# A routed feed-forward in one Trainium2 kernel: choice of experts behind the output's add, ranks a step later, part of the sends in the next block

## The chip, the cores and the metric

The kernel runs on one core of one Trainium2 chip. The metric is the device time of one execution in microseconds, as the median of several runs. The engines are TensorE (PE), VectorE (DVE), ScalarE (ACT), GpSimd (POOL) and SyncE (SP); each runs its own program, and they meet at semaphores.

## The reference, cut to what matters

The model is a two-layer decoder on x of 4096 tokens by 128 channels. All of it is computed in one launch. The change touches its last perceptron, its last routed layer, and (in one layout) the routed layer of layer 0:

```python
# last lines of the second cross attention, x_out is its output, h a perceptron of 4*128
h = gelu(_ln(x_out, ln3_g, ln3_b) @ li2_w + li2_b)
x = x + (... + h @ li3_w + li3_b)
# the last feed-forward, 8 experts, 2 for each token, on flat = layernorm(x)
logits = flat @ Wr.T
weights, ids = top_k(logits, 2)
weights = softmax(weights)
h = einsum('nc,efc->nef', flat, W1)          # efc: 8 x 512 x 128
act = h[..., :256] * silu(h[..., 256:])
out = einsum('nec,ne->nc', einsum('nef,ecf->nec', act, W2), router_weights)
x = x + out
```

## The kernel before, in words

The 4096 tokens lie in `xres` as 32 tiles of 128 tokens (one token per partition). The last two stages are `mlp_route` (names `s5n_`, the perceptron of the cross attention and the routing of the layer that follows) and `sparse` (names `m6_` and `m_`, the routed layer itself). `sparse` also computes the routed layer of layer 0 (`m1_`), early in the program.

**`mlp_route`** works on N = 8 groups of G = 4 tiles in a loop of N + 3 steps. All five programs are written out by hand, and the order of the calls in each step is the order on the engine. A group `t` goes through it as follows. `front(t)` normalises it (DVE, with POOL's `norm.root` for the inverse root), `turn(t)` transposes it (PE), `turn_in(t)` scales it into `xT` (ACT), `hid(t)` and `out(t)` are the two dense products (PE, 8 and 32 records of the trace), the Gelu lies between them (ACT). `carry(t)` adds the residual and the bias to `xres`, and `take(t)` adds the product. `rnorm.stats`, `rnorm.root` and `rnorm.scaled` normalise the sum into `row`, the rows that are sent. `rturn(t)` and `logits(t)` give the scores of the 8 experts, `choose(t)` finds the two best (13 short DVE operations), `ranks(t)` counts by products with constant matrices how many tokens before each one chose the same expert, and `slots(t)` makes the addresses `idx` from them. Then POOL sends the group: 8 indirect DMAs (4 tiles, 2 experts) of 128 rows of 130 floats, to `sorted` in DRAM (`m6r_row` to `sorted` in the trace). In step `t` of the loop, DVE does

```python
choose(t - 3); carry(t); take(t - 1); slots(t - 3)
rnorm.stats(t - 1); norm.stats(t + 2); rnorm.scaled(t - 1); front(t + 2)
```

and PE `hid(t)`, `turn(t + 1)`, `rturn(t - 2)`, `ranks(t - 3)`, `out(t - 1)`, `logits(t - 2)`. POOL does the roots of `t - 1` and `t + 2`, then the sends of group `t - 3`; these wait for `slots(t - 3)` by the semaphore `slotted`, and for ACT's shares. `out(t - 1)` signals `take` by the semaphore `out`. At the end DVE makes from the counts a map of which 256 rows and which expert each tile of the next stage takes.

**`sparse`** waits for the map and for all 64 sends, and then runs a loop of J = 40 tiles of W = 256 rows with B = 8 buffers. SP issues for each tile the rows (`m_xin`), and its expert's `w1` and `w2` (`m_w`), once `scaled(j - 8)` has freed the buffer. PE transposes (`m_turnP`), multiplies by `w1` (`m_hidP`) and by `w2` (`m_yP`), DVE scales the result and makes its addresses (`m_to`, the last of a tile, L3230), and POOL puts it back with two indirect DMAs into `parts`, of 8192 rows of 128 floats. When all are put, SP reads `parts` back in 16 DMAs (8 groups, 2 experts), and DVE adds them to `xres`. A last block stores `xres` with one DMA of 2 MB.

Row number and token are tied by an iota: token n * 128 + p (tile n, partition p) has the row number n * 128 + p in `parts`, so that a partition's tiles lie 128 rows apart there; and the 256 rows of a tile are read as rows p and p + 128 for partition p:

```python
sp.dma_start(xin[s][:], xs[bass.ds(r, W), :].rearrange("(r p) c -> p r c", p=P)).then_inc(came[s], 16)
halves = acc[0:2 * CAP, :].rearrange("(k n p) c -> p k n c", k=2, p=P)
```

Of the kernel before, what the change touches and what calls it, by code (L numbers as in the profile page):

```python
# [22 lines left out]
CAP = NB * L  # L23

# [860 lines left out]
class Routed:  # L885
# [3 lines left out]
    def __init__(self, sc):  # L889
        self.row = sc.sb("row", [P, 2, NT, C + 2])  # L890
        self.map_row = sc.sb("map_row", [P, CAP // 128 + 8], I32)
        self.map_own = sc.sb("map_own", [P, CAP // 128 + 8], I32)
        self.sent = sc.sem("sent")
        self.map_ready = sc.sem("map_ready")


def mlp_route(nc, xres, ident, dram, tag, mtag, src, rt, store):
# [13 lines left out]
    row, map_row, map_own = rt.row, rt.map_row, rt.map_own  # L911
    with ExitStack() as ctx:
# [31 lines left out]
        idx = sc.sb("idx", [P, 2, NT], U32)  # L944
# [30 lines left out]
        def _(pool):  # L975
# [6 lines left out]
            pool.iota(row[:, :, :, C], pattern=[[CAP, 2], [P, NT]], base=0, channel_multiplier=1, **exact).then_inc(S["consts"], 1)  # L982
# [11 lines left out]
            for t in range(N + 3):  # L994
# [4 lines left out]
                if of(t, 3):  # L999
                    r = t - 3  # L1000
                    pool.wait_ge(S["doubled"], r + 1)
                    pool.wait_ge(S["shared"], 2 * r + 2)
                    pool.wait_ge(S["slotted"], r + 1)
                    for i in range(r * G, r * G + G):
                        for k in range(2):
                            nc.gpsimd.indirect_dma_start(xs, bass.IndirectOffsetOnAxis(idx[:, k, i:i + 1], 0), row[:, k, i, :],
                                                         None).then_inc(rt.sent, 16)

        @block.scalar
        def _(ac):  # L1010
# [9 lines left out]
            for t in range(N + 3):  # L1020
                if t + 1 < N:
                    turn_in(t + 1)
                if t < N:
                    wait(ac, S["out"], t - 1)
                    for c in range(H):
                        ac.wait_ge(S["hidden"], t * H + c + 1)
                        nc.scalar.activation(act[t % 2][:, c, :], hidP[c][:], ACT.Gelu, bias=b1[:, c:c + 1]).then_inc(S["acted"], 1)
                if of(t, 2):
# [6 lines left out]
                if of(t, 3):  # L1035
                    r = t - 3
# [6 lines left out]
        def _(pe):  # L1043
# [51 lines left out]
            for t in range(N + 3):  # L1095
                if t < N:
                    hid(t)
                if t + 1 < N:
# [3 lines left out]
                if of(t, 3):  # L1102
# [9 lines left out]
        def _(ve):  # L1112
# [56 lines left out]
            for t in range(N + 3):  # L1169
                if of(t, 3):  # L1170
                    choose(t - 3)
                if t < N:
                    carry(t)
# [1803 lines left out]
def sparse(nc, xres, ident, dram, tag, glu, store, src=None, rt=None):  # L2977
# [14 lines left out]
    with ExitStack() as ctx:  # L2992
# [6 lines left out]
        if not rt:  # L2999
# [49 lines left out]
                 "gated", "acted", "summed", "scaled", "added")  # L3049
# [24 lines left out]
        def _(sp):  # L3074
            if rt:
                sp.wait_ge(rt.map_ready, 2)
                sp.wait_ge(rt.sent, 16 * 2 * NT)
# [4 lines left out]
            for j, s, q, first, last in tiles(sp):  # L3082
                wait(sp, S["scaled"], j - B + 1)
                r = sp.value_load(entry(map_row, j), min_val=0, max_val=E * CAP + E * W - W)  # L3084
                e = sp.value_load(entry(map_own, j), min_val=0, max_val=E - 1)  # L3085
                sp.dma_start(xin[s][:], xs[bass.ds(r, W), :].rearrange("(r p) c -> p r c", p=P)).then_inc(came[s], 16)  # L3086
                sp.dma_start(w1[s][:], dram[tag + "w1"][:, bass.ds(e, 1), :, :].rearrange("p e k h -> p (e k) h")  # L3087
                             ).then_inc(came[s], 16)
                sp.dma_start(w2[s][:], dram[tag + "w2"][:, bass.ds(e, 1), :, :].rearrange("p e k c -> p (e k) c")  # L3089
                             ).then_inc(came[s], 16)  # L3090
# [358 lines left out]
```

## Time and profile before

| | |
|---|---|
| median of 3 runs | 3299.97 us (3291.67 to 3302.93) |
| profiled execution, own time | 3303.45 us |
| its span | 3301.6 us |
| TensorE clock granted over the span | 0.86 |
| PE busy | 2544.8 us (77%) |
| DVE busy | 2213.1 us (67%) |
| ACT busy | 1537.4 us (47%) |
| POOL busy | 899.7 us (27%) |
| 16 DMA engines | 128.30 MB, mean 39 GB/s |
| `mlp_route` (from its first product) | about 2931 to 3117 us |
| loop of the last `sparse` | 3117 to 3272 us |
| reading back, adds, store | 3272 to 3301.6 us |

The shares are means over a dozen stages that each have their own limit. The change lies in the last 370 us, and in a layout of the early routed layer (loop 880 to 1043 us, reading back to 1062 us). What counts is which wait ends last in these stretches.

### The profile page before, as it was taken

The numbers are of one execution on the slowest core, as the hardware profiler recorded it, in microseconds if no ns is written. First come the engines' busy times: TensorE is split into PE (matmuls) and PEld (weight loads), VectorE is DVE, ScalarE is ACT, GpSimd is POOL, SyncE is SP. The second block draws the span as 40 slices with busy tenths as digits, with TensorE's granted clock in tenths as the row PEclk, the third lists the DMA queues.
The fourth block names the chain that finished last, engine by engine and source line by source line (L and its number), as shares of the span: only waits on it lengthen the run. The fifth ranks groups of instructions, "written<-read, shape, count | busy, mean of one in ns | idle before, by whom it ended". The sixth has DMA issues, their size and how long they took to land. (4 is left out here: it accounts for less than half of the span.)

```text
span 3301.6 us, 52250 instructions
## 1 busy us (share of the span) xinstructions
PE 2544.8 (77%) x16201; PEld 1866.0 (57%) x16201; DVE 2213.1 (67%) x4511; ACT 1537.4 (47%) x4292; POOL 899.7 (27%) x1265
## 2 busy tenths in 40 slices
PE   3888888873296999989933797999998689977485
PEld 2555665552295666656621585666665556655374
DVE  4999999982023677766767524788886389955344
ACT  4666666631021677765522222677774245433111
POOL 4334344423453000003210411111110133314453
PEclk8888888885698999999966668999998989988697
DMA  9300000000374000000000300000000000000266
GB/s 352 125 0 0 0 0 0 0 0 22 111 222 141 1 0 0 0 7 1 0 7 0 63 1 16 1 1 0 0 0 8 16 1 0 0 8 22 68 180 179
DMA packets 107797, 128.30 MB, mean 39 GB/s; under 512 B 30281, under 2 KB 80273, under 8 KB 103570
## 3 DMA queue, kind: packets, MB, share of 16 engines
q1 hardware_dynamic: 98450, 107.66, 10.7%
q0 software_dynamic: 9216, 19.02, 1.7%
q8 instruction: 67, 1.10, 0.1%
q14 instruction: 64, 0.52, 0.1%
HBM read 69.23 MB, written 57.41 MB: 38 GB/s over the span
## 5 line engine op out<-in xcount | busy, mean ns | idle before, releaser
L676 DVE TENSOR_TENSOR_SCAN s_state<-s_decay,s_state 128x4096 f32<-128x4096 f32 x32 | 278.0, 8688 | 35.1 <-ACT s_decay L474 35.1
L572 PE MATMUL s_ysumP<-s_state,ident 128*128 128x256 f32 x1024 | 288.0, 434 | 1.4 <-DVE s_state L686 1.4
L1493 ACT ACTIVATE s5a_prob<-s5a_scoreP,s5a_nmax 128x256 f32<-128x256 f32 x512 | 235.2, 474 | 68.2 <-DVE s5a_nmax L1667 67.8
L572 PEld LDWEIGHTS s_ysumP<-s_state,ident 128*128 128x128 f32 x1024 | 217.9, 223 | 35.3 <-DVE s_state L686 1.9
L517 PE MATMUL s_bcP<-s_bc,s_sel 96*128 96x256 bf16 x768 | 152.2, 339 | 106.8 <-DVE s_state L686 93.0
L1493 ACT ACTIVATE s2s_prob<-s2s_scoreP,s2s_nmax 128x128 f32<-128x128 f32 (+1 forms) x512 | 208.2, 423 | 45.2 <-DVE s2s_nmax L1665 44.1
L474 ACT ACTIVATE s_decay<-s_delta,s_aneg 128x255 f32<-128x255 f32 x512 | 210.0, 493 | 33.1 <-DVE s_delta L653 33.0
L3141 POOL DMA_INDIRECT parts<-m_y,m_to x160 | 153.2, 957 | 170.3 <-DVE m_y L3232 136.1
L1667 DVE TENSOR_REDUCE s5a_nmax<-s5a_scoreP 128x4 f32<-128x1024 f32 x128 | 156.6, 1224 | 43.7 <-PE s5a_scoreP L1588 41.1
L517 PEld LDWEIGHTS s_bcP<-s_bc,s_sel 96*128 96x128 bf16 x768 | 82.7, 117 | 176.5 <-DVE s_state L686 125.5
L1665 DVE TENSOR_REDUCE s2s_nmax<-s2s_scoreP 128x2 f32<-128x256 f32 (+1 forms) x256 | 130.6, 552 | 63.6 <-PE s2s_scoreP L1583 59.5
L3325 PE MATMUL m_hidP<-m_xT,m_w 128*128 128x256 f32 x640 | 155.5, 387 | 0.1
L1676 DVE COPY s2s_probT<-s2s_probP 128x768 f32<-128x768 f32 x128 | 122.3, 956 | 46.5 <-PE s2s_probP L1598 46.3
L686 DVE TENSOR_TENSOR s_state<-s_state,s_bcP 128x1024 f32<-128x1024 f32 x128 | 149.3, 1217 | 3.3
L664 DVE TENSOR_TENSOR s_state<-s_bcP,s_du 128x1024 f32<-128x1024 f32 x128 | 147.6, 1217 | 1.2
L1588 PE MATMUL s5a_scoreP<-s5a_k,s5a_q 32*128 32x256 f32 x1024 | 147.7, 406 | 0.8 <-ACT s5a_k L1473 0.8
L365 POOL TENSOR_TENSOR s_pos<-s_pos,s_lost 128x512 f32<-128x512 f32 x16 | 144.6, 9038 | 1.3
L1678 DVE TENSOR_TENSOR s5a_probT<-s5a_probP,s5a_mask 128x768 f32<-128x768 f32 x128 | 122.1, 954 | 29.5 <-PE s5a_probP L1598 27.0
L3318 PE MATMUL m_turnP<-ident,m_xin 128*128 128x128 f32 x160 | 33.2, 291 | 139.9 <-DMA m_w<-in_m_w 137.8
L3288 ACT ACTIVATE m_act<-m_hidP 128x1024 f32<-128x1024 f32 x40 | 40.9, 1023 | 211.5 <-PE m_hidP L3325 195.3
L3333 PEld LDWEIGHTS m_yP<-m_w,m_act 128*128 128x128 f32 x960 | 119.2, 192 | 12.8 <-DVE m_act L3224 7.4
L3333 PE MATMUL m_yP<-m_w,m_act 128*128 128x128 f32 x960 | 120.4, 275 | 7.2 <-DVE m_act L3224 7.2
(643 smaller groups left out, 6318.4 us busy)
## 6 DMA issues: line engine op xcount, KB each, us to landing
sorted<-blank SPq DMA_DIRECT2D x32, 1105.0 KB, 28.1
m_w<-in_m_w SPq DMA_DIRECT2D x120, 256.0 KB
m_xin<-sorted SPq DMA_DIRECT2D x80, 130.0 KB
m_w<-in_m_w SPq DMA_DIRECT2D x40, 128.0 KB
m_row<-parts SPq DMA_DIRECT2D x16, 256.0 KB, 5.3
s_mats<-s_scratch SPq DMA_DIRECT2D x4, 1024.0 KB, 12.4
m6r_row<-parts SPq DMA_DIRECT2D x16, 256.0 KB, 5.1
parts<-m_y,m_to POOLq DMA_INDIRECT x160
```

The costliest lines, as they stand in the source:

```text
L474: ins = nc.scalar.activation(decay[c][:, n, 1:], delta[:, c, 1:], ACT.Exp, scale=aneg[:, c, n:n + 1])
L517: ins = nc.tensor.matmul(bcP[k % 2][:, n, :], sel[:, line + n, :], bc3[s][:], start=True, stop=True)
L572: ins = nc.tensor.matmul(ysumP[:, c, :], ident[:], state[s][:, c, n, :], start=(n == 0), stop=(n == NS - 1))
L664: ins = nc.vector.tensor_tensor(state[s][:, c, GN * g:GN * g + GN, :], bcP[g % 2][:], du[:, c:c + 1, :].to_broadcast([P, GN, L]), ALU.mult)
L676: nc.vector.tensor_tensor_scan(cells, flat(decay[c]), cells, 0.0, ALU.mult, ALU.add).then_inc(S["scanned"], 1)
L686: nc.vector.tensor_tensor(part, part, bcP[k % 2][:], ALU.mult).then_inc(S["bc_used"], 1)
L1493: ins = nc.scalar.activation(prob[i][:, h, a:b], scoreP[i][:, h, a:b], ACT.Exp, bias=nmax[:, p % 4, h, r:r + 1], accum_out=den[s][:, r, 2 ...
L1588: ins = nc.tensor.matmul(scoreP[i][:, h, a:b], q[rows_of(h), c, r * P:r * P + P], k[rows_of(h), c, :], start=True, stop=True)
L1667: ins = nc.vector.tensor_reduce(nmax[:, p % 4, :, :].rearrange("p h r -> p (h r)"), scoreP[i][:].rearrange("p h (r k) -> p (h r) k", r=2), ...
L3141: nc.gpsimd.indirect_dma_start(acc, bass.IndirectOffsetOnAxis(to[s][:, i:i + 1], 0), y[s][:, i, :], None).then_inc(put[s], 16)
L3325: ins = nc.tensor.matmul(hidP[s % 2][:, c, :], w1[s][:, c, :], xT[s % 2][:], start=True, stop=True)
L3333: ins = nc.tensor.matmul(yP[s % 2][:, i * C:i * C + C], act[s % 2][:, k, i * P:i * P + P], w2[s][:, k, :], start=(k == 0), stop=(k == HK - 1))
```

## The change

It does this:

- **DVE in `mlp_route`**: `choose(t - 3)` is moved from the step's head to behind `take(t - 1)`; `slots` works a step later, on `t - 4`, at the step's head; `carry(t)` goes to the step's end. The loop has a step more.
- **PE**: `ranks(t - 4)` and `out(t - 1)` now stand right behind `hid(t)`, `turn` and `rturn` behind them. `logits(r)` waits for `chosen(r - 1)` and no longer for `slotted(r - 1)`.
- **ACT**: the Gelu of `t` comes before `turn_in(t + 1)`, and the shares of `t - 4` take the place of those of `t - 3`.
- **POOL**: a step sends group `t - 4`. The last LATE = 2 groups, 16 sends, are taken out of the loop and sent at the head of `sparse`'s POOL program, behind the change of blocks.
- **SP in `sparse`** (the routed one alone): the weights of the first 8 tiles are issued before the wait for the sends.
- **Partition order** (both `sparse`): the token in partition p, tile n has the row number p * 32 + n, so that the four rows which a partition reads back for a group lie next to each other in DRAM; and a tile's partition p reads rows 2p and 2p + 1 (one run of 260 floats and not two of 130).
- **Store**: each group of the output is stored by a DMA of 256 KB as soon as its adds are done, inside `sparse`; the last block is gone.

```diff
+LATE = 2
...
+    def send(self, nc, xs, i):
+
+        for k in range(2):
+            nc.gpsimd.indirect_dma_start(xs, bass.IndirectOffsetOnAxis(self.idx[:, k, i:i + 1], 0), self.row[:, k, i, :],
+                                         None).then_inc(self.sent, 16)
...
-            pool.iota(row[:, :, :, C], pattern=[[CAP, 2], [P, NT]], base=0, channel_multiplier=1, **exact).then_inc(S["consts"], 1)
+            pool.iota(row[:, :, :, C], pattern=[[CAP, 2], [1, NT]], base=0, channel_multiplier=NT, **exact).then_inc(S["consts"], 1)
...
-                if of(t, 3):
-                    r = t - 3
+                if of(t, 4):
+                    r = t - 4
                     pool.wait_ge(S["doubled"], r + 1)
                     pool.wait_ge(S["shared"], 2 * r + 2)
                     pool.wait_ge(S["slotted"], r + 1)
-                    for i in range(r * G, r * G + G):
-                        for k in range(2):
-                            nc.gpsimd.indirect_dma_start(xs, bass.IndirectOffsetOnAxis(idx[:, k, i:i + 1], 0), row[:, k, i, :],
-                                                         None).then_inc(rt.sent, 16)
+                    for i in range(r * G, r * G + G if r < N - LATE else r * G):
+                        rt.send(nc, xs, i)
...
-                wait(pe, S["slotted"], r)
+                wait(pe, S["chosen"], r)
...
                 if t < N:
                     hid(t)
+                if of(t, 4):
+                    ranks(t - 4)
+                if of(t, 1):
+                    out(t - 1)
                 if t + 1 < N:
                     turn(t + 1)
                 if of(t, 2):
                     rturn(t - 2)
-                if of(t, 3):
-                    ranks(t - 3)
-                if of(t, 1):
-                    out(t - 1)
-                if of(t, 2):
                     logits(t - 2)
...
+            carry(0)
+            for t in range(N + 4):
+                if of(t, 4):
+                    slots(t - 4)
                 if of(t, 1):
                     take(t - 1)
                 if of(t, 3):
-                    slots(t - 3)
+                    choose(t - 3)
...
+                if t > 0 and t < N:
+                    carry(t)
...
                 sp.wait_ge(rt.map_ready, 2)
+                for s in range(B):
+                    weights(s, sp.value_load(entry(map_own, s), min_val=0, max_val=E - 1))
                 sp.wait_ge(rt.sent, 16 * 2 * NT)
...
+                sp.dma_start(xin[s][:], xs[bass.ds(r, W), :].rearrange("(p r) c -> p r c", p=P)).then_inc(came[s], 16)
+                if not (rt and isinstance(j, int) and j < B):
+                    weights(s, sp.value_load(entry(map_own, j), min_val=0, max_val=E - 1))
...
-            halves = acc[0:2 * CAP, :].rearrange("(k n p) c -> p k n c", k=2, p=P)
+            halves = acc[0:2 * CAP, :].rearrange("(k p n) c -> p k n c", k=2, p=P)
...
+            if final is not None:
+                tiled = final.rearrange("(t p) c -> p t c", p=P)
+                for t in range(N):
+                    sp.wait_ge(S["added"], t + 1)
+                    sp.dma_start(tiled[:, t * G:t * G + G, :], group(xres, t)).then_inc(S["stored"], 16)
+                sp.wait_ge(S["stored"], 16 * N)
...
-            if not rt:
+            if rt:
+                for i in range(NT - LATE * G, NT):
+                    rt.send(nc, xs, i)
+            else:
                 send(pool)
...
-        with nc.Block() as block:
-            @block.sync
-            def _(sp):
-                sp.dma_start(out.rearrange("(t p) c -> p t c", p=P), xres[:]).then_inc(gone, 16)
-                sp.wait_ge(gone, 16)
```

DVE in a middle step of `mlp_route` before, from the end of `choose` to the statistics of the group just taken (`outP` is the product, `found` and `idx` belong to `slots`, `s_xo` is the residual):

```order
L1150 TENSOR_TENSOR s5n_both<-s5n_hot 128x32
L1152 TENSOR_TENSOR s5n_apart<-s5n_top 128x4
L1127 TENSOR_TENSOR xres<-xres,s_xo 128x512
L1128 TENSOR_TENSOR xres<-xres,s5n_b 128x512
L1133 TENSOR_TENSOR xres<-xres,s5n_outP 128x512
L1157 TENSOR_TENSOR s5n_found<-s5n_hot,s5n_gateP 128x64
L1158 TENSOR_REDUCE s5n_at<-s5n_found 128x8
L1159 SCALAR_TENSOR_TENSOR s5n_idx<-s5n_which,s5n_at 128x2x4
L1161 TENSOR_REDUCE s5n_part<-s5n_both 128x8
L1162 TENSOR_TENSOR s5n_run<-s5n_run,s5n_part 128x8
L88 TENSOR_TENSOR s5n_r_cell<-s5n_r_cell 128x1
```

The same place in the changed kernel, where the 13 operations of `choose` stand between the add and the statistics (its middle ones are left out here):

```order
L1132 TENSOR_TENSOR xres<-xres,s5n_b 128x512
L1161 TENSOR_TENSOR s5n_found<-s5n_hot,s5n_gateP 128x64
L1162 TENSOR_REDUCE s5n_at<-s5n_found 128x8
L1163 SCALAR_TENSOR_TENSOR m6r_idx<-s5n_which,s5n_at 128x2x4
L1165 TENSOR_REDUCE s5n_part<-s5n_both 128x8
L1166 TENSOR_TENSOR s5n_run<-s5n_run,s5n_part 128x8
L1137 TENSOR_TENSOR xres<-xres,s5n_outP 128x512
L1144 TENSOR_REDUCE s5n_top<-s5n_gateP 128x4
...
L1154 TENSOR_TENSOR s5n_both<-s5n_hot 128x32
L1156 TENSOR_TENSOR s5n_apart<-s5n_top 128x4
L89 TENSOR_TENSOR s5n_r_cell<-s5n_r_cell 128x1
```

`slots` has moved ahead of the add and `choose` behind it; the statistics come after both as before. POOL from the last group's root on, before (L144 is the root, L1006 a send, L3133 the first instruction of `sparse`):

```order
L144 TENSOR_TENSOR s5n_r_rstd<-s5n_r_var,s5n_r_power 128x4
L1006 DMA sorted<-m6r_row,s5n_idx 34816x130 x24
L912 UNCONDITIONAL_BRANCH
L101 ISA
L3131 UNCONDITIONAL_BRANCH
L3133 IOTA m_spill 128x16
L3141 DMA parts<-m_y,m_to 10240x128 x80
```

and in the changed kernel:

```order
L145 TENSOR_TENSOR s5n_r_rstd<-s5n_r_var,s5n_r_power 128x4
L901 DMA sorted<-m6r_row,m6r_idx 34816x130 x16
L920 UNCONDITIONAL_BRANCH
L102 ISA
L3147 UNCONDITIONAL_BRANCH
L3149 IOTA m_spill 128x16
L901 DMA sorted<-m6r_row,m6r_idx 34816x130 x16
L3160 DMA parts<-m_y,m_to 10240x128 x80
```

After the last root 24 sends stood before the change of blocks; now 16 stand there and 16 behind it, and the group that was sent in the step before the last root is sent after it.

## Rows read from the trace of the kernel before

**Rows 1.** Windows, columns: window, length, PE, PEld, DVE, ACT, POOL, clock, DMA share, GB/s

```profile
3117.00:3272.00 155.00, 122.64 (x720) 107.35 (x720) 69.92 (x200) 24.73 (x41) 76.73 (x81) 0.94 0.58 171
880.00:1043.50 163.50, 152.11 (x1040) 142.68 (x1040) 44.60 (x160) 40.92 (x40) 76.58 (x80) 0.96 0.65 193
3271.00:3289.00 18.00, 0.00 (x0) 0.00 (x0) 9.75 (x15) 0.00 (x0) 0.00 (x0) 0.50 0.92 236
```

**Rows 2.** Timeline of a step of the perceptron with sends: start, duration, engine, line

```profile
3015.34 1.04 POOL L1006 DMA_INDIRECT sorted<-m6r_row,s5n_idx  x1 [0.18 <-issue]
...
3020.45 3.82 PE L1065 MATMUL s5n_outP<-s5n_w,s5n_act 128*128 128x128 f32 x32
...
3024.76 0.96 POOL L1006 DMA_INDIRECT sorted<-m6r_row,s5n_idx  x1 [0.30 <-issue]
...
3026.81 0.69 DVE L1133 TENSOR_TENSOR xres<-xres,s5n_outP 128x512 f32<-128x512 f32 x1 [6.24 <-remote]
```

**Rows 3.** Timeline of the first step, before any send, and the last group's add

```profile
2957.07 3.74 PE L1065 MATMUL s5n_outP<-s5n_w,s5n_act 128*128 128x128 f32 x32
...
2960.84 0.69 DVE L1133 TENSOR_TENSOR xres<-xres,s5n_outP 128x512 f32<-128x512 f32 x1 [13.68 <-PE s5n_outP L1065]
...
3076.87 0.69 DVE L1133 TENSOR_TENSOR xres<-xres,s5n_outP 128x512 f32<-128x512 f32 x1 [8.35 <-PE s5n_outP L1065]
```

**Rows 4.** Timeline of DVE and POOL between the adds of groups 4 and 5

```profile
3027.41 0.21 DVE L1157 TENSOR_TENSOR s5n_found<-s5n_hot,s5n_gateP 128x64 f32<-128x64 f32 x1
...
3028.32 0.15 DVE L88 TENSOR_TENSOR s5n_r_cell<-s5n_r_cell 128x1 f32<-128x1 f32 x1
...
3032.77 1.04 POOL L1006 DMA_INDIRECT sorted<-m6r_row,s5n_idx  x1 [0.18 <-issue]
...
3033.94 0.18 DVE L1140 TENSOR_REDUCE s5n_top<-s5n_gateP 128x4 f32<-128x32 f32 x1
...
3036.57 0.68 DVE L1127 TENSOR_TENSOR xres<-xres,s_xo 128x512 f32<-128x512 f32 x1
...
3044.26 0.69 DVE L1133 TENSOR_TENSOR xres<-xres,s5n_outP 128x512 f32<-128x512 f32 x1 [6.28 <-remote]
```

**Rows 5.** Timeline from the last send to the first tile of the last routed layer

```profile
3110.67 0.96 POOL L1006 DMA_INDIRECT sorted<-m6r_row,s5n_idx  x1 [0.31 <-issue]
...
3117.81 0.14 POOL L3133 IOTA m_spill<- 128x16 f32 x1 [6.18 <-POOLq L102]
...
3119.35 0.40 SPq L3086 DMA_DIRECT2D m_xin<-sorted  x1
...
3126.05 0.69 PE L3318 MATMUL m_turnP<-ident,m_xin 128*128 128x128 f32 x2 [2.03 <-DMA m_w<-in_m_w]
```

**Rows 6.** Timeline of the loop: DVE's last operation of tiles 11, 14, 17, 39

```profile
3173.04 0.15 DVE L3230 TENSOR_TENSOR m_to<-m_xin,m_spill 128x2 uint32<-128x2 f32 x1
...
3183.93 0.15 DVE L3230 TENSOR_TENSOR m_to<-m_xin,m_spill 128x2 uint32<-128x2 f32 x1
...
3192.84 0.15 DVE L3230 TENSOR_TENSOR m_to<-m_xin,m_spill 128x2 uint32<-128x2 f32 x1
...
3265.34 0.16 DVE L3230 TENSOR_TENSOR m_to<-m_xin,m_spill 128x2 uint32<-128x2 f32 x1 [0.54 <-issue]
```

**Rows 7.** Timeline of SP's queue: the rows of tiles 9 and 19

```profile
3145.63 0.38 SPq L3086 DMA_DIRECT2D m_xin<-sorted  x1
...
3185.01 0.38 SPq L3086 DMA_DIRECT2D m_xin<-sorted  x1
```

**Rows 8.** Timeline of the end: last put, reading back, last add, store

```profile
3269.46 0.96 POOL L3141 DMA_INDIRECT parts<-m_y,m_to  x1 [0.30 <-issue]
3271.78 12.73 SPq L3096 DMA_DIRECT2D m6r_row<-parts  x16
...
3288.94 1.42 DVE L3262 TENSOR_TENSOR xres<-xres,m6r_row 128x512 f32<-128x512 f32 x2 [0.18 <-DMA m6r_row<-parts]
3292.11 0.38 SPq L3429 DMA_DIRECT2D out<-xres  x1
```

More of the change, by code:

```diff
@@ L993, in _ @@
             pool.wait_ge(filled, 32 * BLANKS)
-            for t in range(N + 3):
+            for t in range(N + 4):
                 if of(t, 1):
@@ L1019, in _ @@
             ac.wait_ge(S["loaded"], 64)
-            for t in range(N + 3):
-                if t + 1 < N:
-                    turn_in(t + 1)
+            for t in range(N + 4):
                 if t < N:
@@ L1027, in _ @@
                         nc.scalar.activation(act[t % 2][:, c, :], hidP[c][:], ACT.Gelu, bias=b1[:, c:c + 1]).then_inc(S["acted"], 1)
+                if t + 1 < N:
+                    turn_in(t + 1)
                 if of(t, 2):
@@ L1094, in _ @@
             pe.wait_ge(S["consts"], 8)
-            for t in range(N + 3):
+            for t in range(N + 4):
                 if t < N:
                     hid(t)
+                if of(t, 4):
+                    ranks(t - 4)
+                if of(t, 1):
+                    out(t - 1)
                 if t + 1 < N:
@@ L1168, in _ @@
             ve.wait_ge(S["consts"], 8)
[L1169 to L1173, printed above, removed]
+            carry(0)
+            for t in range(N + 4):
+                if of(t, 4):
+                    slots(t - 4)
                 if of(t, 1):
@@ L2974, in layout5, with sparse @@
     return laid
-def sparse(nc, xres, ident, dram, tag, glu, store, src=None, rt=None):
+def sparse(nc, xres, ident, dram, tag, glu, store, src=None, rt=None, final=None):
     G = 4
@@ L3048, in sparse @@
                  "shares", "chosen", "ranked", "idx_ready", "map_ready", "sent", "xT_turned", "xT_ready", "hidden",
-                 "gated", "acted", "summed", "scaled", "added")
+                 "gated", "acted", "summed", "scaled", "added", "stored")
         S = {n: sc.sem(n) for n in names}
@@ L3074, in _, with weights @@
         def _(sp):
+            def weights(s, e):
+                sp.dma_start(w1[s][:], dram[tag + "w1"][:, bass.ds(e, 1), :, :].rearrange("p e k h -> p (e k) h")
+                             ).then_inc(came[s], 16)
+                sp.dma_start(w2[s][:], dram[tag + "w2"][:, bass.ds(e, 1), :, :].rearrange("p e k c -> p (e k) c")
+                             ).then_inc(came[s], 16)
             if rt:
                 sp.wait_ge(rt.map_ready, 2)
+                for s in range(B):
+                    weights(s, sp.value_load(entry(map_own, s), min_val=0, max_val=E - 1))
                 sp.wait_ge(rt.sent, 16 * 2 * NT)
@@ L3107, in send @@
                       allow_small_or_imprecise_dtypes=True).then_inc(S["consts"], 1)
-            pool.iota(row[:, :, :, C], pattern=[[CAP, 2], [P, NT]], base=0, channel_multiplier=1,
+            pool.iota(row[:, :, :, C], pattern=[[CAP, 2], [1, NT]], base=0, channel_multiplier=NT,
                       allow_small_or_imprecise_dtypes=True).then_inc(S["consts"], 1)
@@ L3374, in stage56 @@
         stage5(nc, xres, ident, dram, rt)
-        sparse(nc, xres, ident, dram, "m6_", True, dram["m6_store"], rt=rt)
+        sparse(nc, xres, ident, dram, "m6_", True, dram["m6_store"], rt=rt, final=dram["out"])
 def lay_out(i, np):
@@ L3409, in build @@
         dram["blank"] = (xs, blank, blanked, filled)
+        dram["out"] = out
         with nc.Block() as block:
```

14 lines of the change are left out of this document (3 added, 11 removed).

## The prediction

> **What bounds the kernel now.** I first read the windows of the stretches that the change touches, to see which of them is full. The early routed layer's loop is PE's: busy 152.1 of 163.5 us, with the DMA engines at 0.65 [rows 1]. The last one's loop is nobody's: PE is busy 122.6 of 155 us and the DMA engines are at 0.58 [rows 1]. The reading back is the DMA engines', at 0.92 and 236 GB/s, with PE idle [rows 1]. Then I read the timelines of the last 370 us for who waits for whom.
>
> In the perceptron the surprise is in [rows 2]. PE's product of group 4 starts at 3020.45 and is over 3.82 us later, at 3024.27, by its modelled end. DVE's add, which waits for nothing else and had been idle for 6.2 us, starts at 3026.81, 2.5 us after. What does end just before it is POOL's run of eight sends, from 3015.34 to 3024.76 + 0.96 = 3025.72. The distance from the run's end to the add is 1.09 us here, and about as much at the next two groups. With no send about, the add follows the product at once: 2957.07 + 3.74 = 2960.81, and the add is at 2960.84 [rows 3]. So I read: **the signal of a dense product is held while POOL sends back to back, and comes about 1.06 us after the run.** The step is then a chain: add, statistics, root, run of eight sends (10.38 us), 1.1 us, next add. By rows: add 3026.81, first send 3032.77 (5.96 us), add 3044.26, a step of 17.45 us [rows 2, 4]. PE and DVE have slack in it.
>
> In the loop of the last routed layer the same appears in a smaller form: between tiles 11 and 14 DVE's last operation moves by 3183.93 − 3173.04 = 10.89 us, 3.63 us a tile, and this spacing repeats to the hundredth from tile 5 on (four times); POOL puts six DMAs back to back in each such period. From tile 17 to 39 it is (3265.34 − 3192.84)/22 = 3.30 us a tile [rows 6]: there PE waits for SP's transfers, the sends have gaps, and nothing is held.
>
> **The change part by part**, against the profiled execution's own 3303.45 us, which is 3.5 us above the median of the runs.
>
> *Steps without sends (groups 0 to 3).* The sends of group 0 move a step later, so that the add of group 3 is no longer behind a run. A step's DVE work is some 11.4 us and PE's 10 to 11 us at full clock; by this the adds come at about 2960, 2969, 2979 and 2992 (three steps of 9 to 13 us). Before, the fourth came at 3009.4, after two longer steps and a run of sends. This gains 17 us, but it is gain only if the sends that follow are not what sets the end.
>
> *Steps with sends.* `choose` takes 3036.57 − 3033.94 = 2.63 us and now stands between the add and the statistics; `slots`, 3028.32 − 3027.41 = 0.91 us, leaves that place [rows 4]. From the add to the first send it is then 5.96 + 1.69 = 7.65 us, and the step 7.65 + 10.38 + 1.06 = 19.1 us where it was 17.45. In the last steps, with no statistics of a coming group, it is 17.6. From the add of group 3 at 2992.3: adds at 3011.4, 3030.5, 3048.1 and 3065.7. The last was at 3076.87 [rows 3], so 11 us are gained by here.
>
> *The end of the stage.* But now groups 4 to 7 are unsent at that add, where it was 5 to 7: 32 sends, not 24. Two groups go at once: first send at 3065.7 + 6.2 = 3071.9, end at 3092.7. The map is made in that time. The change of blocks took 3117.81 − 3111.63 = 6.2 us [rows 5], so the other 16 start at 3098.9 and, at twice the 10.38 us of a run, end at 3119.7, while before all had ended at 3111.63. SP waits for them: with a landing of 1.4 us (from the last put's end at 3270.42 to the next issue at 3271.78 [rows 8]) and a register load, rows are issued at about 3122.1, where the first was issued at 3119.35 [rows 5]. The weights are there by then (8 x 384 KB in 20 us), which saves their two issues before the second tile's rows, so the second transposes, at 3126.05 before [rows 5], are at about 3126. PE's first product stands behind them. **Sum to the first product: 0.** The 11 us and the early weights pay for 8 more sends and for a barrier that no longer covers anything but itself.
>
> *The loop.* With eight tiles of weights there SP is some 7 us ahead at tile 8. PE then doesn't wait for transfers from tile 17 on, POOL's puts stay back to back, and the pattern of 3.63 us a tile holds on: 22 x (3.63 − 3.30) = **+7 us** (bounds: −5, if the lead is simply kept to the end; +11, if it holds on from tile 8).
>
> *Partition order.* The rows of a tile come as one run of 1040 bytes in place of two of 520. In the early loop this is beside PE's work, 0 us. The reading back now has its four rows side by side in DRAM, but on the SBUF side they still land 130 floats apart. I take the runs to stay 512 bytes: 0 to −2 us early, **−1**. If they became 2048 bytes, it would be 5 us less in each of the two reads.
>
> *The store.* Last add ends 3290.36, store issued 3292.11, end 3301.6: 1.75 + 9.5 us [rows 8]. Now seven of eight parts are stored beside the reads; but the engines are 0.92 busy there [rows 1], so that 2 MB at 236 GB/s, some 8 us, push the reads. The end comes 2 to 6 us earlier: **−3.5**.
>
> Sum: 3303.45 + 0 + 7 − 1 − 3.5 = 3306; by the runs' median, **3302 us**.
>
> **Against a rule.** The rows show the add 1.1 us behind POOL's run, three times of three. The Trainium skill, SBUF — State Buffer (Who interferes with whom), says that PE and ACT never wait on anyone; only DVE and GpSimd share a port. By that rule PE's product isn't late for the sends' sake, and some other thing orders these rows; the first rival is what it would give, and the trace does not agree with it as I read it.
>
> **The rivals.**
>
> *1. The signal isn't held in the new order.* For it: short products' signals (the transposes', the ranks') get through in the middle of a run, and `out` now stands elsewhere in it. Against: three of three. The four steps with sends then take what POOL needs, two roots and the run, some 13.4 us, in place of 19.1, 19.1, 17.6 and 17.6: −20 us in front of the last 16 sends. The loop gives 0 in place of +7 (its pattern is the same thing), the ends −4.5: 3303.45 − 20 − 4.5 = 3279, by the median **3275**. A half way, held for some groups alone, gives 3280 to 3295.
>
> *2. Slower: the loop goes at the pace at which buffers come free.* In the stretch with the pattern SP's issues for tiles 9 to 19 are (3185.01 − 3145.63)/10 = 3.94 us apart [rows 7], since each waits for `scaled` of eight tiles before, and it loses its lead over PE there. If the pattern spreads and each release is late by it, tiles 8 to 39 go at 3.94 and not at the 3.33 they had: +19 in place of +7. This decides if the lead at tile 8 is eaten within ten tiles. 3303.45 + 19 − 4.5 = 3318, by the median **3314**. Against it: a tile's 658 KB, its puts included, take 2.8 us at the 236 GB/s of the reading back [rows 1].
>
> *3. It does not do what it says*: the store by groups and the partition order bring nothing (a gain of 0 for −4.5). Then 3306. It lies in the first case's range.
>
> **How the numbers follow.** About 0.3%, 10 us, is what a measurement of this kernel can tell from no change: faster is below 3290, slower above 3310. The held signal as above, with the bounds of the loop and of the ends (3290 to 3310): 0.50. Not held, or held in part: 0.33. Slower: 0.17. The likeliest case's own range is 3290 to 3309. Since the first rival has a third, the range reaches to its middle, 3272, and to 3313 at the other end. Faster 0.34, same 0.48, slower 0.18.
>
> **What would show it.** Right: adds of groups 3 to 7 some 19 us apart with each about 1.1 us behind a run's end; first product of the last routed layer within 3 us of 3126.5; tiles 3.63 us apart to the thirties; last stores issued right behind the last add. Wrong: steps with sends of 13 to 15 us, and the last routed layer starting 15 us or more earlier (rival 1); SP waiting for `scaled` with tiles 3.9 us apart (rival 2); a reading back of under 14 us (runs of 2048 bytes).

## The result and the profile after

The changed kernel takes 3274.81 us (median of 6 runs, 3269.45 to 3283.2) against 3295.82 us for the kernel before (6 runs): a ratio of 0.9945, 95% interval 0.9926 to 0.9964. That is 12 to 24 us faster, where 3302 was forecast, with no difference that a measurement can tell as the likeliest outcome. 3274.81 is where the first rival stood (3275), though not for its reason; it lies inside the forecast range (3272 to 3313) only because that range had been stretched down for this rival, so that much is luck. The profiled execution has a span of 3272.3 us (3301.6 before).

The part ahead of the perceptron is not touched but for one layout, and its length scatters from run to run: the perceptron began at 2902.7 to 2931.0 us in the 17 profiles of this study. So I count from that start (POOL's first instruction of the stage, 2931.0 before, 2925.8 after):

| us | before | after | forecast of the difference | measured |
|---|---|---|---|---|
| perceptron's start to add of group 3 | 78.4 | 55.4 | -17 | -23.0 |
| adds of group 3 to 7 | 67.5 | 66.4 | +6 | -1.1 |
| add of group 7 to first product of the last routed layer | 49.6 | 57.6 | +11 | +8.0 |
| that product to the last tile's last DVE operation | 138.8 | 136.3 | +7 | -2.5 |
| from there to the end | 36.3 | 30.7 | -3.5 | -5.6 |
| **sum** | 370.6 | 346.4 | +3.5 | **-24.2** |

The rest, 5.2 us, is the earlier start of the stage, the scatter just named. In the early routed layer reading back and adds took 18.8 us before and after.

The windows of the changed kernel, in the columns of [rows 1] and for the same three stretches (the loop of the last routed layer, that of the early one, the reading back):

```profile
3100.00:3242.00 142.00, 125.22 (x720) 110.98 (x720) 68.41 (x199) 23.34 (x40) 73.62 (x77) 0.93 0.55 163
876.80:1040.40 163.60, 152.88 (x1040) 143.20 (x1040) 44.58 (x160) 40.97 (x40) 76.83 (x80) 0.96 0.64 193
3247.00:3265.00 18.00, 0.00 (x0) 0.00 (x0) 10.60 (x16) 0.00 (x0) 0.00 (x0) 0.50 1.03 270
```

The loops have not changed their character. Beside the reading back the stores now run: 270 GB/s where there were 236.

A step with sends in the changed kernel, in the timeline; it answers to [rows 2, 4]:

```profile
2998.41 0.96 POOL L901 DMA_INDIRECT sorted<-m6r_row,m6r_idx  x1 [0.30 <-issue]
2999.07 0.69 DVE L1137 TENSOR_TENSOR xres<-xres,s5n_outP 128x512 f32<-128x512 f32 x1 [4.47 <-remote]
...
3002.13 0.19 DVE L1154 TENSOR_TENSOR s5n_both<-s5n_hot 128x32 f32<-128x32 f32 x1
...
3002.46 1.84 PE L1084 MATMUL s5n_gateP<-s5n_wr,s5n_rowT 128*128 128x8 f32 x8 [4.37 <-DVE s5n_both L1154]
...
3004.16 5.82 PE L1062 MATMUL s5n_hidP<-s5n_xT,s5n_w 128*128 128x512 f32 x8
...
3006.76 1.04 POOL L901 DMA_INDIRECT sorted<-m6r_row,m6r_idx  x1 [0.18 <-issue]
...
3010.86 3.82 PE L1070 MATMUL s5n_outP<-s5n_w,s5n_act 128*128 128x128 f32 x32
...
3014.51 0.60 PE L1055 MATMUL s5n_turnP<-ident,s5n_xn 128*128 128x128 f32 x4
...
3016.73 0.69 DVE L1137 TENSOR_TENSOR xres<-xres,s5n_outP 128x512 f32<-128x512 f32 x1 [4.68 <-remote]
...
3017.44 0.78 ACT L1019 ACTIVATE s5n_xT<-s5n_turnP,s5n_ln 128x512 f32<-128x512 f32 x1 [6.73 <-remote]
```

Read it as PE's chain: add 2999.07, `choose` ends 3002.3 with `both`, PE's `logits` had waited 4.37 us for it, `hid` stands behind `logits`, then `ranks` and the product, which ends at 3014.67 by its modelled end. Its add starts 2.06 us later, at 3016.73, during the last send of the run. So the signal is held as before. It is the signal that is late, not PE and not DVE: PE goes on to its transposes at once (3014.51), and ACT, idle for 6.73 us, sees the end of these transposes (3015.11) only at 3017.44. But `logits <- both` is the wait I had not read: **PE has no slack in this step.** With `out` directly behind `hid` and `ranks`, everything on PE's way from one add to the next is there: 0.6 (add) + 2.6 (`choose`) + 1.8 + 5.8 + 1.1 + 3.8 us, and 2 us of hold.

The end of the changed kernel, in the columns of [rows 8]:

```profile
3247.44 12.11 SPq L3106 DMA_DIRECT2D m6r_row<-parts  x16
...
3259.59 6.64 SPq L3111 DMA_DIRECT2D out<-xres  x8
...
3264.06 1.42 DVE L3281 TENSOR_TENSOR xres<-xres,m6r_row 128x512 f32<-128x512 f32 x2 [0.17 <-DMA m6r_row<-parts]
```

From the first reading DMA to the last add's end it is 18.0 us (18.6 before), so the stores cost the reads nothing that shows, and the end comes 6.8 us behind the last add, where it was 11.2. All 8 stores are issued after the 16 reads, on the same queue.

### The profile page after: what moved, and what is told of

It is laid out like the page before. It is cut to its first block and busy times, and to the rows that moved or that the text cites. A ratio compares the mean times of both kernels' runs of the same rounds, so it can differ in the third digit from the quotient of the medians.

```text
span 3272.3 us, 52245 instructions
## 1 busy us (share of the span) xinstructions
PE 2526.3 (77%) x16201; PEld 1854.9 (57%) x16201; DVE 2212.4 (68%) x4511; ACT 1538.3 (47%) x4290; POOL 901.2 (28%) x1265
## 5 line engine op out<-in xcount | busy, mean ns | idle before, releaser
L573 PEld LDWEIGHTS s_ysumP<-s_state,ident 128*128 128x128 f32 x1024 | 218.3, 224 | 35.6 <-DVE s_state L687 1.8
L3344 PE MATMUL m_hidP<-m_xT,m_w 128*128 128x256 f32 x640 | 162.0, 399 | 1.9 <-DVE m_xT L3237 1.7
L1683 DVE TENSOR_TENSOR s5a_probT<-s5a_probP,s5a_mask 128x768 f32<-128x768 f32 x128 | 122.1, 954 | 31.5 <-PE s5a_probP L1603 29.0
L3337 PE MATMUL m_turnP<-ident,m_xin 128*128 128x128 f32 x160 | 32.4, 286 | 130.9 <-DMA m_w<-in_m_w 97.4
L3344 PEld LDWEIGHTS m_hidP<-m_xT,m_w 128*128 128x128 f32 x640 | 122.2, 201 | 18.0 <-issue 2.0
```

Of the source, the lines that this page charges most:

```text
L573: ins = nc.tensor.matmul(ysumP[:, c, :], ident[:], state[s][:, c, n, :], start=(n == 0), stop=(n == NS - 1))
L3344: ins = nc.tensor.matmul(hidP[s % 2][:, c, :], w1[s][:, c, :], xT[s % 2][:], start=True, stop=True)
```

## Experiments

Fifteen kernels ran, on three chips: e1 to e4 on one (call it X), e5 to e8 on a second (Y), e9 to e15 on a third (Z). Each is compared with the kernel before on its own chip. Which chip the two kernels of the first result ran on is not on record. Stage lengths are those of the table's first rows: F is the perceptron's start to the first product of the last routed layer, L its loop, T the end. Each of these lengths is from one profile of its kernel.

### e1 to e4: which part of the change brings the gain, and the sends taken out of the loop

e1 takes the old order of the steps on all engines (ACT, POOL's three steps and the wait of `logits` for `slotted` go back with it), with all else as changed; in short form, DVE and PE:

```diff
-            carry(0)
-            for t in range(N + 4): slots(t - 4); take(t - 1); choose(t - 3) ...; carry(t)
+            for t in range(N + 3): choose(t - 3); carry(t); take(t - 1); slots(t - 3) ...
-                hid(t); ranks(t - 4); out(t - 1); turn(t + 1); rturn(t - 2); logits(t - 2)
+                hid(t); turn(t + 1); rturn(t - 2); ranks(t - 3); out(t - 1); logits(t - 2)
```

> The changed kernel with the step order of the perceptron as before (choose ahead of the add, ranks and sends three steps back, turn ahead of the product); the two late groups, early weights, rows and store as changed. Theory A (the order is the gain: it starts the steps without sends warm and lets the runs of sends begin at the fourth group's add): the first product of the last routed layer comes 20 to 23 us later than in the changed kernel, counted from the stage's start, and the whole is at or above the kernel before (3296 to 3302). Theory B (the late sends, weights and store are the gain): it stays within 6 us of the changed kernel's 3275.

> The changed kernel with no late groups (all 32 last sends ahead of the change of blocks) and the first tiles' weights issued with their rows, as before. Theory A: 16 sends end at the same distance, then 14.9 us from the last send to the first product as in the kernel before, where the changed kernel has 4.9 (block) + 5.8: +4 us to the first product. The loop 0 to +3 us longer. In all +4 to +7 us over the changed kernel. Theory B: more than +12 us.

> The changed kernel without the early weights alone. First product after the last send's end 9.6 us and not 5.8: +3.9 us; loop from first product to last tile +0 to +3 us by the lead that is lost (my prediction had said that losing the lead shortens the loop by 7).

> All eight groups sent behind the change of blocks, none in the loop. If a dense product's signal is held by sends back to back: each add follows its product within 0.1 us, and steps from the add of group 3 on take 12 to 13 us, not 17.7; the add of group 7 comes 102 us after the stage's start, not 121.8. If the signal is late for another reason (the product itself is slow in coming there): adds stay 1 to 2.5 us behind the modelled end of the product, and the steps stay over 15 us. The end is later by some 37 us in both, for 64 sends stand alone.

e2 sets `LATE = 0` and issues weights with the rows; e3 only does the latter; e4 sets `LATE = 8`.

| | median us | ratio to before, 95% | F | L | T |
|---|---|---|---|---|---|
| e1 old order | 3256.69 | 0.9966 (0.9947 to 0.9986) | 186.1 | 115.2 | 31.0 |
| e2 no late group, no early weights | 3252.09 | 0.9956 (0.9933 to 0.9978) | 175.9 | 120.5 | 30.8 |
| e3 no early weights | 3249.19 | 0.9944 (0.9922 to 0.9966) | 175.1 | 120.9 | 31.1 |
| e4 all sends late | 3301.35 (1 run) | | 229.1 | 115.7 | 31.3 |

Two expectations missed. e1 was to lose all of the gain; by the ratio it keeps more than half (0.34% of the 0.55 to 0.58% that the changed kernel gains). e3 loses 5 us in the loop against e1 and e4, which have the early weights on the same chip, where 0 to 3 were expected. The larger surprise was the chip: the kernel before takes 3267.22 us here (20 runs) and not 3296, and **in no trace of chip X is a signal of PE held.** In e3, with runs of sends, the adds of groups 3 to 7 are 16.1, 14.4, 14.4 and 12.5 us apart, each right behind its product; in e4, with no sends in the loop, 14.4, 14.4, 16.0 and 12.5. So where nothing is held, the sends don't set the step at all. My expectation of e4 (12 to 13 us a step) was a miss: without sends and without a hold the step is still over 14 us, so another chain must set it. e2 against e3 says that late groups by themselves bring 0.8 us to F: of the 4 us that e2 was to lose, and lost against e6 (175.9 and 172.2), nearly all is the weights'. They can only be issued early because sends are still to come.

### e5 to e8: both kernels on one other chip, `choose` moved, the store undone

```diff
e7:
-                if of(t, 3):
-                    choose(t - 3)
                 if of(t, 1):
                     ve.wait_ge(S["out_used"], t)
                     rnorm.stats(nc, ve, st, t - 1, lambda g: tile(xres, t - 1, g))
                 if t + 2 < N:
                     norm.stats(nc, ve, st, t + 2, lambda g: tile(src, t + 2, g))
+                if of(t, 3):
+                    choose(t - 3)
```

> The kernel before, unchanged, on the chip of this call, for its trace. The last four kernels ran on another chip than the first two, and there no signal of PE was held by POOL's runs. If this chip doesn't hold them either: adds of groups 4 to 6 within 0.1 us of the product's end, steps of some 16.5 us where they were 17.45, the last loop some 20 us shorter than 139 us. If it holds them, the trace repeats that of before within 2 us a stage.

> The changed kernel, unchanged, on the same chip as the kernel before. If the held signal is what the change works around, the gain is smaller on a chip that holds none. If the gain is in the order of the steps and in the store (theory A), first product some 16 us earlier from the stage's start and 5.5 us less at the end on either chip, 18 to 24 us in all.

> The changed kernel with choose(t - 3) moved behind the statistics of t - 1 and t + 2, so that its 2.6 us no longer stand between the add and the sends. My prediction's term: each of the four steps with sends loses up to 2.6 us, where the chain add, statistics, root, run, held signal sets the step: first product 5 to 10 us earlier. Rival: where nothing is held, PE's chain (logits wait for chosen) or DVE's own sum sets the step, and it gains under 2 us or loses.

> The changed kernel with one DMA of 2 MB in a block of its own at the end, as before, everything else as changed. From the last tile to the end 36.2 us and not 30.7 (5.5 us more). If the partition order had its part in that (rival), only 2 to 4 us more.

| | median us | ratio to before, 95% | F | L | T |
|---|---|---|---|---|---|
| e5 before | 3258.63 (1 run; 3263.36 in 25 others) | | 182.6 | 122.9 | 35.6 |
| e6 changed | 3242.82 | 0.9942 (0.9919 to 0.9964) | 172.2 | 115.8 | 30.9 |
| e7 choose later | 3260.15 | 1.0006 (0.9981 to 1.0031) | 188.1 | 116.3 | 31.5 |
| e8 one store | 3248.55 | 0.9956 (0.993 to 0.9983) | 171.9 | 115.5 | 36.0 |

Chip Y holds no signal either, and the ratio is the same as in the first result. The gain is made of other pieces: F -10.4 (some 16 were expected), L -7.1, T -4.7. e8 gives back 5.1 us of T and nothing else: that is the store's whole price, as my term had it (-3.5, 2 to 6). Against e6, e1 has an F longer by 13.9 us, and e3 one longer by 2.9 and an L longer by 5.1: the order of the steps is worth some 14 us, the early weights some 8, the store 5 (e1 and e3 are from chip X, which like Y held nothing). These are sizes from single profiles. By the ratios the three are 8, 1 and 5 us, each with an interval of some 10 us to either side, so the times alone settle none of them.

e7 tests my chain, on a chip where nothing is held. If add, statistics, root and sends set the step, 2.6 us less between add and sends must help. It costs 15.9 us in F and the whole gain in time. PE and DVE in e7, in the timeline:

```profile
3007.21 1.85 PE L1084 MATMUL s5n_gateP<-s5n_wr,s5n_rowT 128*128 128x8 f32 x8 [4.21 <-DVE s5n_both L1154]
```

```profile
3002.16 0.69 DVE L1137 TENSOR_TENSOR xres<-xres,s5n_outP 128x512 f32<-128x512 f32 x1 [2.66 <-PE s5n_outP L1070]
3006.88 0.19 DVE L1154 TENSOR_TENSOR s5n_both<-s5n_hot 128x32 f32<-128x32 f32 x1
```

The add comes at once, `both` 4.7 us later, and PE waits 4.21 us for it, where it waits 2.57 us in e6. So `choose` stands behind the add for PE's sake: `logits` writes the PSUM tile (`gateP`) that `choose` reads, hence its wait for `chosen`.

### e9 to e11: PE's wait taken away, the rows undone, the run of sends broken

```diff
e9, PE:
                 hid(t)
+                logits(t - 3)
                 ranks(t - 4)
                 out(t - 1)
                 turn(t + 1)
                 rturn(t - 2)
-                logits(t - 2)
e11, POOL:
                     for i in range(r * G, ...):
+                        if i == r * G + 3 and t < N:
+                            pool.wait_ge(S["out"], t + 1)
                         rt.send(nc, xs, i)
```

> The changed kernel with PE's logits(t - 3) right behind hid(t) in place of logits(t - 2) at the step's end. Theory C, formed after the last runs: the step is PE's own chain (product, add, choose, logits, hid, ranks, product), since logits writes the PSUM bank that choose reads and waits for it 2.6 us, and hid stands behind it and runs at half clock for the idle time. Then these 2.6 us go, hid takes 3.7 us more often, and steps from the fourth add on take 13 to 14 us (POOL's two roots and its run) in place of 14.4 to 16 (17.7 where signals are held): first product 5 to 10 us earlier. Theory of my prediction (the chain through statistics and the run of sends sets the step): no change, within 1.5 us.

> The changed kernel with tokens and rows numbered tile by tile as before, and a tile's rows read as two runs of 520 bytes. Early routed layer: loop and reading back within 1 us. Reading back of the last one: first issue to last add's end within 0.5 us of 18.0 to 18.4, if its runs are 512 bytes in both, as the packets of the changed kernel say (8192 of 512 bytes for both reads); 2 us longer if rows side by side in DRAM help. Loop 0 to +2 us for 5120 packets more.

> The changed kernel, POOL waiting for the product's signal after six of the eight sends of a run. If this chip holds signals during a run (as the first did): the signal comes some 1.1 us after the sixth send's end and not at or after the eighth's, so that adds come 1 to 1.5 us earlier in three steps. If it holds none (as the last two): adds come as in the changed kernel there (14.4 to 16 us apart), and the runs end up to 2 us later.

| chip Z | median us | ratio to before, 95% | F | L | T | adds of groups 3 to 7 apart |
|---|---|---|---|---|---|---|
| e9 logits next | 3260.12 | 0.9863 (0.9829 to 0.9897) | 162.0 | 139.9 | 32.4 | 11.3, 12.8, 12.5, 14.0 |
| e10 old rows | 3272.18 | 0.9905 (0.9877 to 0.9932) | 179.4 | 137.5 | 32.0 | 17.9, 17.7, 17.7, 13.1 |
| e11 pause | 3268.59 (1 run) | | 174.9 | 142.0 | 29.7 | 16.5, 16.4, 14.9, 12.5 |

Chip Z holds signals again, as the first traces did (before: 3298.57 us), and e10's perceptron is that of the first trace to a tenth. e10 shows that the numbering by partition brings nothing that these runs can tell: reading back to last add 18.2 us (18.0 changed, 18.6 before), the early layer's 19.1 (18.8). The packets say why: 12288 of 512 bytes in the window of reading back and store, before and after alike, and 10128 fewer in all, as 80 tiles are read in packets of 1040 bytes.

PE in e9:

```profile
2993.33 0.60 PE L1055 MATMUL s5n_turnP<-ident,s5n_xn 128*128 128x128 f32 x4
2993.77 0.60 PE L1077 MATMUL s5n_outP<-ident,m6r_row 128*128 128x128 f32 x4
2994.80 3.70 PE L1062 MATMUL s5n_hidP<-s5n_xT,s5n_w 128*128 128x512 f32 x8 [0.43 <-ACT s5n_xT L1019]
2998.34 0.95 PE L1084 MATMUL s5n_gateP<-s5n_wr,s5n_rowT 128*128 128x8 f32 x8
```

The wait is 0.43 us, `hid` takes 3.70 us where it took 5.82, and F is 17.4 us shorter than in e10, more than the 5 to 10 that I had expected. Theory C holds: **the step was PE's chain with a wait for `choose` in it**. The clock is part of it. Windows of the changed kernel (three steps with sends, then the `hid` of the step shown above) and of e9 (four steps), in the columns of [rows 1]:

```profile
2981.20:3034.50 53.30, 39.77 (x202) 29.11 (x200) 29.27 (x144) 21.97 (x33) 29.80 (x29) 0.81 0.09 31
3004.20:3009.80 5.60, 5.60 (x9) 2.36 (x10) 4.95 (x21) 3.18 (x4) 4.33 (x5) 0.62 0.04 12
```

```profile
2983.50:3027.00 43.50, 34.61 (x215) 27.25 (x213) 33.37 (x169) 23.82 (x38) 30.94 (x30) 0.92 0.11 38
```

In `hid` the granted clock is 0.62, that is, most of it is run at the lower level of 1.2 GHz (0.5); over the steps it is 0.81, with PE busy 39.8 of 53.3 us. In e9 it is 0.92, with PE busy 34.6 of 43.5 us and no wait of several us ahead of `hid`.

e11 shows that the held signal is real. POOL and DVE in e11:

```profile
2990.29 0.96 POOL L901 DMA_INDIRECT sorted<-m6r_row,m6r_idx  x1 [0.30 <-issue]
...
2992.13 0.69 DVE L1139 TENSOR_TENSOR xres<-xres,s5n_outP 128x512 f32<-128x512 f32 x1 [3.12 <-PE s5n_outP L1072]
2992.37 0.96 POOL L901 DMA_INDIRECT sorted<-m6r_row,m6r_idx  x1 [1.11 <-PE s5n_outP L1072]
```

The product ended at 2991.62, the sixth send at 2991.25. The add follows the product in 0.5 us where it took 2, and the steps are shorter by 0.6 to 2.8 us than in e10. POOL, which waits for the same signal, goes on 0.24 us after DVE.

### e12 to e15: what holds the signal, what it costs in the loop, and the best version

```diff
e13 and e15, POOL in the last loop:
                 for i in range(R):
+                    if rt and i == 1 and j + 3 <= J:
+                        pool.wait_ge(S["hidden"], j + 3)
```

> All sends behind the change of blocks once more, for a chip that holds signals. If the sends hold them: no add is late to its product by more than 0.1 us, and the adds of groups 4 to 7 come 14 to 16 us apart as on the chip that held none, not 17.7. If the product is slow by itself there: 1.8 to 2.5 us late as with sends. On a chip that holds none it repeats the earlier run and tells nothing new.

> The changed kernel; in the last loop POOL waits between a tile's two puts for PE's hidden product two tiles on. Where signals are held, runs of four to six puts can't form: the loop takes 118 to 130 us from first product to last tile and not 136 to 142. If the wait itself costs as much as the hold (rival), it stays over 135 us. Where none is held: 115 to 118 us, as without it.

> Logits behind hid once more. Theory C: steps with sends of 11 to 14 us and the first product 162 us after the stage's start on a chip that holds signals, 162 to 166 us on one that holds none (172 there without this edit).

> Both edits. Effects add: first product as in e14, loop as in e13. On a chip that holds signals 30 to 35 us below the changed kernel, on one that holds none 6 to 10 us below.

| chip Z | median us | ratio to before, 95% | F | L | T |
|---|---|---|---|---|---|
| e12 all sends late | 3335.64 (1 run) | | 235.5 | 142.2 | 31.3 |
| e13 pause in the loop | 3258.68 (1 run) | | 179.2 | 130.9 | 32.2 |
| e14 logits next, again | 3261.97 | 0.9915 (0.9885 to 0.9945) | 163.1 | 140.1 | 31.1 |
| e15 both edits | 3248.81 | 0.9877 (0.9815 to 0.994) | 161.4 | 132.0 | 30.2 |

e12 is the clean one. PE and DVE with no send about, on the chip that holds signals:

```profile
2992.19 3.82 PE L1070 MATMUL s5n_outP<-s5n_w,s5n_act 128*128 128x128 f32 x32
...
2999.44 1.03 PE L1084 MATMUL s5n_gateP<-s5n_wr,s5n_rowT 128*128 128x8 f32 x8 [2.56 <-DVE s5n_both L1154]
3000.33 5.38 PE L1062 MATMUL s5n_hidP<-s5n_xT,s5n_w 128*128 128x512 f32 x8
```

```profile
2996.04 0.69 DVE L1137 TENSOR_TENSOR xres<-xres,s5n_outP 128x512 f32<-128x512 f32 x1 [2.66 <-PE s5n_outP L1070]
```

Product's end 2996.01, add 2996.04; the adds of groups 3 to 7 are 16.0, 14.4, 16.1 and 12.5 us apart. So it is the sends that hold the signal, and on this chip they cost 1.8, 3.3, 1.7 and 0.6 us a step. The rest of the step is PE's chain, the same on all chips: e4 on chip X has steps of 14.4, 14.4, 16.0 and 12.5 us. (F is 6 us longer in e12 than in e4 for another reason: PE's hidden product comes 11.7 us behind the last send and not 5.7, the second tile's rows being late.)

The loop shows the same on a larger scale. Windows from first product to last tile: changed kernel (first trace, then chip Y), and e13:

```profile
3105.24:3241.59 136.35, 124.05 (x717) 110.20 (x716) 67.58 (x197) 23.34 (x40) 73.21 (x77) 0.94 0.56 166
```

```profile
3101.80:3217.60 115.80, 115.08 (x718) 105.82 (x716) 67.32 (x197) 23.89 (x40) 73.01 (x77) 0.99 0.67 195
```

```profile
3093.70:3224.60 130.90, 119.87 (x718) 105.89 (x716) 68.17 (x196) 23.90 (x40) 72.21 (x76) 0.99 0.56 172
```

Where nothing is held the loop is PE's, busy 115.1 of 115.8 us. Where signals are held it is 20 us longer. Here is one such tile of the changed kernel in its first trace:

```profile
3188.29 1.89 PE L3344 MATMUL m_hidP<-m_xT,m_w 128*128 128x256 f32 x8
...
3193.75 1.08 ACT L3304 ACTIVATE m_silu<-m_hidP 128x512 f32<-128x512 f32 x2 [5.69 <-PE m_hidP L3344]
```

ACT has been idle for 5.69 us and starts 3.57 us after PE's product has ended, while POOL puts six times in a row. In the traces with a hold it is only PE's signals that come late: in the loop ACT starts up to 3.7 us after a product that it waits for, but DVE never more than 0.12 us after ACT, and PE never more than 0.13 us after DVE. e13 wins back 5 to 11 us of that (130.9 against 136.3 to 142.2 in the other traces of changed kernels with a hold), less than the 6 to 24 that I had expected: runs of three to six puts still form, and signals are still held by up to 2.5 us. e15 adds both edits and has the lowest median of all on chip Z, 0.9877 of the kernel before. By the ratio e9, measured against other runs of the kernel before, stands no worse (0.9863), and the intervals overlap. e15 is 26 us below the first result's 3274.81, where 30 to 35 were expected. Its interval and e14's overlap, so that in time alone the loop's part isn't settled, though the stage's length says 8 us (132.0 against 140.1).

## Why the prediction was wrong

**The step that failed** is the chain of a step with sends: "The step is then a chain: add, statistics, root, run of eight sends (10.38 us), 1.1 us, next add ... PE and DVE have slack in it." Its pieces were right one by one. In the changed kernel add to first send is 7.69 us (7.65 forecast; 2.63 − 0.91 is 1.72 and not 1.69, which changes nothing) and the run 10.27. But the hold isn't a fixed 1.06 us behind the run: the adds of groups 4 and 5 came 0.3 us before the run's end, that of 6 1.2 us behind it, and that of group 7, whose product ended 3.4 us before the run did, wasn't held. And the chain that sets the step is PE's: add, `choose`, `logits`, `hid`, `ranks`, product (e7, e9, e12). The trace of before had a PE chain of the same length, in these lines:

```profile
3028.23 1.85 PE L1079 MATMUL s5n_gateP<-s5n_wr,s5n_rowT 128*128 128x8 f32 x8 [3.96 <-DVE s5n_idx L1159]
...
3029.93 6.02 PE L1057 MATMUL s5n_hidP<-s5n_xT,s5n_w 128*128 128x512 f32 x8
...
3037.78 3.82 PE L1065 MATMUL s5n_outP<-s5n_w,s5n_act 128*128 128x128 f32 x32
```

From the add at 3026.81 PE waits for `slots` (3.96 us idle), then comes `logits`, `hid`, the short products and `out`, which ends at 3041.60: 14.8 us, and 2.66 of hold make up the 17.45. "PE and DVE have slack in it" was false there already. I took the chain with the odd thing in it for the one that counts. In the table this is the second row, 7 us.

**Steps without sends** came out 6 us better than my -17. I had costed them at DVE's 11.4 us and PE's 10 to 11, but started the first add at 2960, as before. It came 5.6 us earlier from the stage's start (24.2, not 29.8; on chip Y 24.2, not 27.1). By the trace this is because ACT does the Gelu ahead of the next `turn_in`, and PE's second `hid` no longer waits for it; no run turns back this edit alone. Before and after:

```profile
2950.14 6.65 PE L1057 MATMUL s5n_hidP<-s5n_xT,s5n_w 128*128 128x512 f32 x8 [3.02 <-ACT s5n_act L1027]
```

```profile
2942.70 3.70 PE L1062 MATMUL s5n_hidP<-s5n_xT,s5n_w 128*128 128x512 f32 x8 [1.01 <-ACT s5n_xT L1019]
```

I had left ACT's edit out of the sum. The same product takes 3 us more behind that wait, at a granted clock of 0.55 and not 1.00.

**The end of the stage**: 8.0 us for +11. The two runs took 20.0 and 19.9 us (20.8 each), the change of blocks, up to the first send behind it, 5.6 (6.2), and the last send to the first product 5.8 (6.8). Right in kind, each term some tenths too large.

**The loop** failed in sign: "+7" was -2.5, and on chip Y -7.1. The 3.63 us a tile of [rows 6] did not spread; the changed kernel runs at 3.30 us a tile from tile 5 to 39. My reading that from tile 17 on "nothing is held" was also false: in the trace of before DVE starts on tile 33 1.9 us after PE's product, and ACT on tile 37 1.5 us after it, and without a hold the same 22 tiles take 2.94 us each (e5) and not 3.30. On a chip without the hold the early weights gain 5 us in the loop (e3 against e1 and e4). My bound of -5 stood for that case, and -7.1 is beyond it.

**Store and rows**: 5.1 us for -3.5 (e8), and 0 for -1 (e10). The third rival was half right: the store brings its part, the rows nothing.

**The rivals.** The first had the time and not the mechanism, so its hit is luck: the signal is held in the new order too. Where it isn't (chips X and Y), the steps take 14.4 to 16 us and not the 13.4 it said, since PE's chain sets them. By the rule of the Trainium skill, SBUF — State Buffer (Who interferes with whom), PE and ACT never wait on anyone. That is a rule on ports, and the traces don't contradict it: PE runs on during the hold (its transposes start at 3014.51, at the product's end), and what comes late is its signal, 0.03 us behind the product without sends and some 2 us with them on chip Z (e12, e10). I had been wrong to set the rule against the rows. What differs between the chips was not tried and stays open, and so does why some signals within a run get through.

## What to carry to other kernels

List the waits of the busiest in-order engine in a step and add its chain from one release to the next before you believe a chain through other engines; two chains of equal length look alike in a trace, and only moving a piece tells them apart. A result that another engine must read before a buffer is free belongs as far from its reader as the program allows: one short product moved behind the next large one (e9) took 17 us off the stage on chip Z; on a chip that holds nothing it was not tried. Before you build on an oddity of one trace, look whether a second chip shows it.

## What the runs showed of the hardware

- On one of three chips (Z), and in the first two traces, signals of PE's products come late while POOL issues indirect DMAs back to back: by 1.8 to 2.7 us in three steps of the kernel before and of the changed one, by up to 3.7 us in the last loop. On the two others the signals of the perceptron's large products come 0.01 us behind them, by the semaphore events of the traces. In the same loops no engine starts more than 0.13 us (POOL 0.28, in all traces) behind a signal of DVE or ACT. Where in the run the product ends does not settle it: a product that ended 3.4 us before the run's end was signalled at once (changed kernel, group 7), one that ended 7.0 us before it 4.2 us late (e14, group 6).
- The kernel before takes 3298.57 us on chip Z and 3267.22 and 3263.36 on the two others. Its first trace, with a hold, and the one of chip Y differ by 16 us in the last loop (138.8 against 122.9 us) and by 13 ahead of it (195.5 against 182.6). Of these 13, 5.9 lie ahead of the first send, where no signal is late.
- A pause of POOL after six of eight sends lets the signal through within 0.5 us (e11).
- Stores of 2 MB begun behind the reads of 4 MB raised the rate from 236 to 270 GB/s. The reads and adds took 18.2 us with them and 18.8 without (e6, e8).
- The same `hid` of 8 records takes 3.70 us in the seven steps of e9 from the second on. In the changed kernel it takes 3.7 us from the second to the fifth, and 5.5 to 6.2 us in the last three, which stand behind waits of PE of 2.6, 4.4 and 4.6 us (granted clock 0.62 in the one shown); the fifth stands behind a wait of 2.6 us too.
